# Two expert layers of a one-core kernel: up products per batch as rows are turned, routing placed among them, a bias taken into the shared expert's down product, and later folds

## The reference, cut to what matters

```python
# second layer (E=8 routed experts, I=256, top 2) and one shared expert
s = softmax(z @ gate_w.T); idx = top2(s + gate_b); comb = s where chosen, else 0
up_e = z @ w1[e] + b1[e];  c_e = z @ w3[e] + b3[e];  q = up_e * c_e
g, l = q[..., ::2], q[..., 1::2]
g = min(g, 7); l = clip(l, -7, 7); h_e = g * sigmoid(1.702 * g) * (l + 1)
y = sum_e comb_e * (h_e @ w2[e] + b2[e]) + (shared: h_s @ sw2 + sb2)
x = x + layernorm(y)

# third layer (E=8, F=512, top 2, weights of the two chosen normalised)
y = sum_e comb_e * (silu(z @ W1[e].T) @ W2[e].T);  x = x + layernorm(y)
```

## Time and profile before

| what | value |
|---|---|
| median of three runs | 2537.59 us (2532.54 to 2545.24) |
| profiled execution, its own time | 2533.08 us |
| its span | 2531.3 us, 46421 instructions |
| PE busy | 1916.8 us (76%) |
| PEld busy | 1318.0 us (52%) |
| DVE busy | 1696.1 us (67%) |
| ACT busy | 1089.0 us (43%) |
| POOL busy | 851.6 us (34%) |
| mean granted TensorE clock | 0.859 |

### The profile page before, as it was taken

One profiled execution on the slowest core, in us unless ns is written; L12 is line 12 of the kernel. 1 busy time (PEld: TensorE's weight loads), 2 busy tenths in 40 slices (PEclk: granted clock), 3 DMA queues, 4 the chain that ended last, 5 costly groups with the idle time before them and its releaser, 6 DMA issues. The chain is left out here.

```text
span 2531.3 us, 46421 instructions
## 1 busy us (share of the span) xinstructions
PE 1916.8 (76%) x16420; PEld 1318.0 (52%) x16420; DVE 1696.1 (67%) x4018; ACT 1089.0 (43%) x2022; POOL 851.6 (34%) x630
## 2 busy tenths in 40 slices
PE   5888886587778876449999846878878747999666
PEld 2555554255555553337777614444444336888444
DVE  4777777676555564668999951788887857223574
ACT  2666664354445542204444421555555412333442
POOL 3000000774455430113344333445454319900211
PEclk8999999799999898659999965698888757999678
DMA  3011110200000000010000046566665432000000
GB/s 104 30 39 40 40 38 2 80 16 16 16 16 16 16 16 1 5 22 11 21 21 16 5 133 172 145 175 174 169 178 166 119 122 89 26 8 1 6 1 19
DMA packets 126969, 144.92 MB, mean 57 GB/s; under 512 B 73222, under 2 KB 100673, under 8 KB 123992
## 3 DMA queue, kind: packets, MB, share of 16 engines
q1 hardware_dynamic: 123542, 132.82, 18.9%
q10 hardware_dynamic: 3266, 9.96, 1.0%
HBM read 94.46 MB, written 40.81 MB: 53 GB/s over the span
## 5 line engine op out<-in xcount | busy, mean ns | idle before, releaser
L454 ACT ACTIVATE l0a_pr<-l0a_sm,l0a_nm 128x512 f32<-128x512 f32 x256 | 185.1, 724 | 142.6 <-DVE l0a_nm L367 142.1
L367 DVE CUSTOM_DVE_ANT_0 l0a_sm<-l0a_ps_s,l0a_tb 128x512 f32<-128x512 f32 x256 | 170.8, 685 | 87.6 <-PE l0a_ps_s L522 84.7
L2609 ACT ACTIVATE l2a_pr<-l2a_ps_s,l2a_nm 128x512 f32<-128x512 f32 x256 | 173.8, 685 | 116.6 <-DVE l2a_nm L2528 115.6
L530 PE MATMUL l0a_ps_p<-top_c_ident,l0a_pr 128*128 128x128 f32 x1024 | 168.9, 288 | 54.4 <-ACT l0a_pT L462 54.2
L530 PEld LDWEIGHTS l0a_ps_p<-top_c_ident,l0a_pr 128*128 128x128 f32 x1024 | 109.3, 142 | 116.5 <-ACT l0a_pr L454 65.1
L2528 DVE TENSOR_REDUCE l2a_nm<-l2a_ps_s 128x2 f32<-128x1024 f32 x128 | 156.7, 1224 | 4.4
L2535 DVE STREAM_TRANSPOSE l2a_tt<-l2a_pr 128x1024 f32<-128x1024 f32 x128 | 158.0, 1234 | 0.1
L1557 POOL TENSOR_TENSOR l1f_h<-l1f_lm,l1f_sg 128x512 f32<-128x512 f32 x72 | 92.5, 1285 | 184.9 <-DVE l1f_lm L1626 184.9
L807 POOL TENSOR_TENSOR l0f_ct<-l0f_raw,l0f_cos_scaled 128x1024 f32<-128x1024 f32 x32 | 76.7, 2397 | 174.0 <-issue 94.2
L1929 ACT ACTIVATE l2f_h<-l2f_ps_h 128x512 f32<-128x512 f32 x128 | 76.5, 598 | 135.8 <-PE l2f_ps_h L1474 129.8
L1684 ACT ACTIVATE l1f_csb<-l1f_ps_c,l1f_b3e 128x512 f32<-128x512 f32 x128 | 88.1, 688 | 106.0 <-PE l1f_ps_c L1474 105.7
(11 more groups left out here) (522 smaller groups left out, 5190.5 us busy)
## 6 DMA issues: line engine op xcount, KB each, us to landing
l2a_rawk<-l_k SPq DMA_DIRECT2D x16, 1024.0 KB, 13.3
l2a_qb<-l_qband SPq DMA_DIRECT2D x16, 768.0 KB
l2a_sb<-l_pband SPq DMA_DIRECT2D x32, 384.0 KB
l_qband<-l2a_staged SPq DMA_DIRECT2D x14, 768.0 KB, 15.1
l0a_tb<-l_bias SPq DMA_DIRECT2D x16, 448.0 KB
l2a_ks<-l_k SPq DMA_DIRECT2D x16, 384.0 KB
l_pband<-l2a_pr SPq DMA_DIRECT2D x32, 192.0 KB, 8.7
l_pband<-l2a_pr SPq DMA_DIRECT2D x32, 144.0 KB, 2.2
```

What stands on the lines that cost most here:

```text
L367: v.tensor_tensor_reduce(sm[j % 4][:, :], ps_s[j % 2][:, :], tb[slot][:, off:off + N][:, ::-1], -1.0, 3e38, ALU.add, ALU.min, nm[:, j % 4: ...
L454: a.activation(pr[j % 4][:, :], sm[j % 4][:, :], ACT.Exp, bias=nm[:, j % 4:j % 4 + 1], scale=-1.0).then_inc(m["p_ready"], 1)
L530: last = pe.transpose(ps_p[j % 2][:, tile(k)], pr[j % 4][:, tile(k)], ident[:, :])
L2609: a.activation(pr[slot][:, 2 * (g % 2) + u, :], ps_s[g % 2][:, u, :], ACT.Exp, bias=nm[:, g % 2, u:u + 1], accum_out=rs[:, n % 2, 2 * (g % ...
```

## The change

In both layers the splitting of turned tokens moves between the normalisations of later batches (`Router.tokens`, `Router.split`), weights are masked or stored before the routing, the logits stand after the last turned batch, and the up products wait only for the split of their own batch. In `l1_ffn` the routing weights are turned after the first batch's up products, four products of 36 columns instead of sixteen of 9; ACT copies them. `b2` is a block tile of 36 rows (zeroed on GpSimd, eight loads), one 36-row product per batch opens the shared expert's down product, which then accumulates; `acc` is begun by a copy of this sum instead of by a start value and an add. TensorE's first pair of experts is written out, the others stay in a loop. In `l2_ffn` the fold loads move from ACT's queue to SP's, behind the first two experts' weights; `wcon` is turned after the third batch's up product; GpSimd waits for the first accumulation before the butterflies.

```diff
 class Router:
+    def split(self, v, ch, b):
+        cols = slice(b * N, (b + 1) * N)
+        v.wait_ge(self.zT_ready, b + 1)
+        ch.link(high_part(v, self.zT_masked[:, cols], self.zT[:, cols]))
+        v.tensor_copy(self.zT_high[:, cols], self.zT_masked[:, cols])
+        v.tensor_tensor(self.zT_low[:, cols], ..., ALU.subtract).then_inc(self.parts_ready, 1)
+
+    def tokens(self, v, ch, xs, weights):
+        for b in range(B + 1):
+            if b < B:
+                self.norm.statistics(v, ch, b, lambda t: xs[:, b * NT + t, :])
+            if b:
...
+                self.norm.normalize(v, ch, b - 1, ...)
+                ch.wait()
+                v.sem_inc(self.zb_ready, 1)
+            if b >= 2:
+                self.split(v, ch, b - 2)
+            if b == B:
+                weights()
+        self.split(v, ch, B - 1)
+
+    def route(self, v, ch, ps_gate, ...):
...
 l1_ffn, sync
-                sp.dma_start(b2[0:E, :], w["b2"]).then_inc(biases, 16)
-                sp.dma_start(b2[E:E + 1, :], w["sb2"]...).then_inc(biases, 16)
+                sp.wait_ge(b2_zero, 1)
+                for t in range(NT):
+                    first = t * (E + 1)
+                    sp.dma_start(b2[first:first + E, t, :], w["b2"]).then_inc(b2_loaded, 16)
+                    sp.dma_start(b2[first + E:first + E + 1, t, :], w["sb2"]...).then_inc(b2_loaded, 16)
...
 l1_ffn, vector
-                r.vector(v, ch, xs, ps_gate, gate_b, gate_b_loaded)
-                v.wait_ge(biases, 16 * (2 * (E + 1) + 2))
+                r.tokens(v, ch, xs, lambda: mask_weights(0, 0))
+                r.route(v, ch, ps_gate, gate_b, gate_b_loaded)
                 v.sem_inc(comb_ready, 1)
-                mask_weights(0, 0)
-                for b in range(B):
-                    v.wait_ge(ct_ready, b + 1)
-                    v.tensor_copy(combT[:, b * N:(b + 1) * N], ps_t[0:E + 1, :]).then_inc(combT_ready, 1)
-                for b in range(B):
-                    v.wait_ge(init_ready, b + 1)
-                    v.tensor_copy(acc[:, b * NT:(b + 1) * NT, :], ps_y[b % 2][:, :, :]).then_inc(acc_done, 1)
+                v.wait_ge(biases, 16 * 2 * (E + 1))
...
+                    if shared:
+                        v.tensor_copy(acc[:, b * NT:(b + 1) * NT, :], ps_y[b % 2][:, :, :]).then_inc(acc_done, 1)
+                        return
...
 l1_ffn, scalar
                 for b in range(B):
                     step(0, b, b3[:, 0, :, :])
+                    if b == 0:
+                        a.wait_ge(ct_ready, 1)
+                        a.copy(combT[:, :], ps_t[0:R, :]).then_inc(combT_ready, 1)
...
 l1_ffn, tensor
-                r.tensor(pe, ps_t, ps_gate)
-                pe.wait_ge(comb_ready, 1)
...
+                r.turn(pe, ps_t)
+                r.logits(pe, ps_gate)
...
                 def down(e, b, slot):
+                    if shared:
+                        pe.wait_ge(combT_ready, 1)
+                        pe.wait_ge(b2_loaded, 16 * 2 * NT)
+                        pe.matmul(ps_y[b % 2]..., combT[:, b * P:(b + 1) * P], b2..., start=True, stop=False)
...
                 for b in range(B):
                     up(0, b, 0)
-                    if b:
+                    if b == 0:
+                        pe.wait_ge(comb_ready, 1)
+                        for k in range(B):
+                            last = pe.transpose(ps_t[0:R, k * P:(k + 1) * P], r.comb[:, k * NT:(k + 1) * NT, :]..., ident)
+                        last.then_inc(ct_ready, 1)
+                    else:
                         down(0, b - 1, 0)
...
 l2_ffn, sync: behind load(0), load(1)
+                sp.dma_start(wcon...); sp.dma_start(fold.up[0]...); sp.dma_start(fold.bu[0]...)
+                for i in range(fold.stages):
+                    sp.dma_start(upw[:, i, :], ...); sp.dma_start(dnw[:, j, :], ...)
 l2_ffn, gpsimd
+                g.wait_ge(acc_done, 1)
                 g.wait_ge(first_loaded, 32)
                 g.wait_ge(dn0_ready, 1)
 l2_ffn, vector
-                store_weights(0, 0)
-                r.vector(v, ch, xs, ps_gate, None, normalize=True)
+                r.tokens(v, ch, xs, lambda: store_weights(0, 0))
+                r.route(v, ch, ps_gate, None, normalize=True)
 l2_ffn, scalar
...
-                r.scalar(a, ps_t)
+                r.turned(a, ps_t)
+                r.exponential(a)
                 for b in range(B):
                     step(0, b)
+                    if b == 2:
+                        a.wait_ge(wcon_ps, 1)
+                        a.copy(fold.dn[0][:, :], ps_t[:, :]).then_inc(dn0_ready, 1)
 l2_ffn, tensor
+                r.turn(pe, ps_t)
                 turn_weights(0, 0, 0)
...
-                r.tensor(pe, ps_t, ps_gate)
-                pe.wait_ge(r.parts_ready, B)
+                r.logits(pe, ps_gate)
                 for b in range(B):
+                    pe.wait_ge(r.parts_ready, b + 1)
                     up(0, b, 0)
                     if b:
                         down(0, b - 1, 0)
+                    if b == 2:
...
```

More of the change, by code:

```diff
@@ L1446, in tensor, with logits @@
             last.then_inc(self.t_ready, 1)
+    def logits(self, pe, ps_gate):
         pe.wait_ge(self.zT_ready, B)
@@ L1735, in down @@
                     n = e * B + b
+                    shared = isinstance(e, int) and e == 0
+                    if not (shared and b < 2):
+                        pe.wait_ge(acc_done, n - 1)
+                    if shared:
+                        pe.wait_ge(combT_ready, 1)
+                        pe.wait_ge(b2_loaded, 16 * 2 * NT)
+                        pe.matmul(ps_y[b % 2][:, :, :].rearrange("p t d -> p (t d)"), combT[:, b * P:(b + 1) * P],
+                                  b2[:, :, :].rearrange("p t d -> p (t d)"), start=True, stop=False)
                     pe.wait_ge(h_ready, n * 2 + 2)
-                    pe.wait_ge(acc_done, n + 3)
                     for t in range(NT):
@@ L1740, in down, with expert @@
                             last = pe.matmul(ps_y[b % 2][:, t, :], h[b % 2][:, k, t * P:(t + 1) * P], w2[slot][:, k, :],
[L1741 removed]
+                                             start=(k == 0 and not shared), stop=(k == 1 and (t == NT - 1 or not shared)))
                     last.then_inc(y_ready, 1)
[L1744 removed]
                 for b in range(B):
                     up(0, b, 0)
[L1747 to L1756 removed]
+                    if b == 0:
+                        pe.wait_ge(comb_ready, 1)
+                        for k in range(B):
+                            last = pe.transpose(ps_t[0:R, k * P:(k + 1) * P], r.comb[:, k * NT:(k + 1) * NT, :].rearrange("p t e -> p (t e)"),
+                                                c["ident"][:, :])
+                        last.then_inc(ct_ready, 1)
+                    else:
+                        down(0, b - 1, 0)
+                def expert(e, slot):
+                    for b in range(B):
+                        up(e, b, slot)
+                        if b == 0:
+                            down(e - 1, B - 1, 1 - slot)
+                        else:
+                            down(e, b - 1, slot)
+                expert(1, 1)
+                expert(2, 0)
+                with pe.Fori(1, E // 2) as i:
+                    expert(i * 2 + 1, 1)
+                    expert(i * 2 + 2, 0)
                 down(E, B - 1, 0)
@@ L1982, in _ @@
                         down(0, b - 1, 0)
+                    if b == 2:
+                        pe.wait_ge(wcon_loaded, 16)
+                        for k in range(fold.chunks):
+                            last = pe.transpose(ps_t[:, k * P:(k + 1) * P], wcon[:, k, :], c["ident"][:, :])
+                        last.then_inc(wcon_ps, 1)
                     if b == 1:
```

98 lines of the change are left out of this document (33 added, 65 removed).

## The result

| | before | changed kernel |
|---|---|---|
| median of four runs | 2535.07 us (2532.51 to 2545.24) | 2492.41 us (2491.69 to 2496.87) |
| profiled execution, its own time (span) | 2533.08 (2531.3) us | 2491.87 (2489.7) us |
| PE busy | 1916.8 us (76%) | 1895.2 us (76%) |
| DVE busy | 1696.1 us (67%) | 1665.9 us (67%) |
| ACT busy | 1089.0 us (43%) | 1090.1 us (44%) |

The time ratio is 0.9834, with an interval of 0.9814 to 0.9854: 42 us faster, give or take 5. The forecast was 2500.2 us within 2491 to 2512, 37.4 us faster. A second set of runs of the same changed kernel gave 2493.97 us, ratio 0.9836 (0.9815 to 0.9856). One execution of the kernel before, in the runs beside e9 to e12, took 4245 us and is left out of their ratios.

A forecast was written before the change was run, and what follows sets the result against it. The order of work in the two expert layers' heads was taken as the bound, not engine busy time. Savings of 15.0 (first layer) and 22.4 (second) make 37.4, taken from the 2537.6 median: 2500.2 us, range 2491 to 2512.

The forecast's parts named there:

- The heads are on the path, the loops keep their length: Both expert layers: time saved ahead of the steady loop moves all that follows, and the steady loops keep their length.
- Layer 1, first up product 19.2 earlier: First expert layer's head: first up product starts at 1123.0 instead of 1142.22, with 3 us of slack for the weights.
- First product 15.6 earlier, routing is what comes next: First expert layer: VectorE must finish routing first, so it takes the first product at 1130.4, 15.6 us earlier.
- From the first to the second batch 8.3, bounds 7.0 and 10.5: First expert layer: first to second batch's first product takes 8.3 us, was 8.26; 7.0 at best, 10.5 at low clock.
- Rival (a): First layer: TensorE's 3 us gap drops the clock, shared expert runs half slow, bias products cost 3.4; 2506.5; chance 0.10.
- Bias products 0.5 in all: First layer's shared expert: four products of 0.86 us each, three hidden where VectorE is behind, the fourth mostly paid: 0.5.
- Layer 2, 22.4: Second expert layer: 22.4 us saved (19.5 to 23.5), first up product 23.0 earlier, logits lasting 7.0, `wcon` transposes costing 0.6.
- The three parts of its first up product: Second layer's head, 23.0 earlier: 12.5 waiting for weights, some 12 of GpSimd slowing VectorE, less the logits' new order.
- The fold loads' place on ScalarE, "the layer's gain would be nearer 15": Second layer's head: with the fold loads left on ScalarE, its copy holds the tokens until 2087; gain nearer 15.
- Butterflies from 44 us on, 67 us of cover: Second layer: butterflies start about 44 us after the layer's start and end 67 us before GpSimd is next wanted.
- (b): Second layer starts less early: single-queue loads late or VectorE slowed before the butterflies; 8 to 15 lost, say 2511; chance 0.09.
- (c): Second layer: third expert's weights arrive late behind 10 MB of fold loads on SP; slower than before, about 2545; chance 0.02.

The follow-up runs named there:

- e9: Kernel before, with one wait added: GpSimd starts the second expert layer's butterflies only after the first accumulation; 2521.31 us, ratio 0.9949.
- e12: The changed kernel run again without an edit; 2493.97 us, ratio 0.9836 against the kernel before.
- e1: Changed kernel with only the first expert layer changed, the second layer as before with the old router; 2522.71 us, ratio 0.9959.
- e2: Changed kernel with only the second expert layer changed, the first layer as before with the old router; 2509.39 us, ratio 0.9896.
- e3: Changed kernel with the 21 fold loads back at the head of ScalarE's queue; 2506.14 us, ratio 0.9881 against the kernel before.
- e6: Changed kernel with each bias product moved ahead of the third half of the next up product; 2493.76 us, ratio 0.9820 against the kernel before.
- e7: Changed kernel with twelve unused products filling TensorE's 3.34 us gap in the first layer; 2493.44 us, ratio 0.9831 against the kernel before.
- e5: Changed kernel without the down biases and their four products; 2494.97 us, ratio 0.9827 against the kernel before.
- e10: Changed kernel with seven unused wide products between the token turnings in each layer's head; 2496.24 us, ratio 0.9838 against the kernel before.
- e4: Changed kernel with `wcon` turned ahead of the logits and butterflies not waiting for the first accumulation; 2497.10 us, ratio 0.9851 against the kernel before.
- e8: Changed kernel with each batch's logits made right after the next batch is turned, in both layers; 2493.08 us, ratio 0.9819 against the kernel before.

## Why the prediction was right, point by point

- **The heads are on the path, the loops keep their length.** Right. Both layers' steady parts are within 0.4 us of before, and layer gains pass through to the kernel (e1, e2).
- **Layer 1, first up product 19.2 earlier.** 19.6, with the weights' slack of 3 us at 2.1.
- **First product 15.6 earlier, routing is what comes next.** 15.7. Right, and the timeline shows it: `comb`, then the product. VectorE's count of steps (13.5 for four statistics, four normalisations and two splits) placed the last turning 13.45 us into layer 2.
- **From the first to the second batch 8.3, bounds 7.0 and 10.5.** 7.8 in five of eight profiles with the gap and 9.2 in three (e1, e3, e6); 6.55 without the gap (e7). The bounds held both. Rival (a) had the mechanism right, a gap drops the clock, and had its extent wrong: the clock is back 2.9 us behind the gap in the changed kernel, 5.9 behind it in e1. The Trainium skill (TensorE: Matmul & The Clock Gate, HAM oscillation), on which that rival leant, tells of waits for DMAs that put the array back to the lower clock for the work behind them. The granted clock of 0.50 from 1130 agrees, here behind a wait of 3.34 us for VectorE, and e7 prices it at 1.0 to 2.2 of the layer.
- **Bias products 0.5 in all.** Wrong: 3.4. This is the mis-sized term, and both factors failed. One product costs TensorE 1.25 (1.06 until the down product starts) rather than 0.86. And the cover was read off one place, the fourth batch of the earlier trace rows, and given to three of the four products, but only two lie ahead of it; these cost 0.3 and 0.5. The other two lie where VectorE already waited for operands in the kernel before, and cost 1.3 each. Rival (a) had the same sum, "paid in full (3.4)", by luck: four in full would be 5.0, and it is two in full and a third of the others. Without the products layer 1 would have gained 16.7, against a forecast of 15.5 ahead of this term.
- **Layer 2, 22.4.** 22.9 to 23.9 when the logits last about 7 us (e2, e5, e6, e10, e12), as the sum had it; 26.5 when they last 4.05. All of these are counted from the 276.05 of one profile; against the 279.42 of the same old code in e1 they would be 3.4 more. The logits' duration was taken as fixed from a row at half clock. That TensorE's clock might rise within them was not in the sum nor among the rivals, and it brings 2.6 of the 4.1 us by which the layer beat the forecast in that execution.
- **The three parts of its first up product.** The prediction put 12.5 on the wait for weights and 12 on GpSimd's interference. Holding the butterflies alone brings 13.4 (e9); the rest of the change brings the remaining 10.7 (33.41 to 22.74). But the wait for weights is not what that was: e3 has the tokens ahead of the weights and the butterflies held, and its first up product stands at 34.23, no earlier than e9's. All of the 10.7 needs the fold loads off ScalarE; statistics that start 12.5 earlier bring nothing while the copy behind them is held. The Trainium skill (SBUF — State Buffer, SBUF: two separate sides) calls the port pair that VectorE and GpSimd share an exclusive lock for the length of an instruction; the trace agrees: a split takes 0.68 alone, a butterfly instruction 1.28, and the four splits beside them took 1.74 to 2.01 in the kernel before, 1.76 in e4.
- **The fold loads' place on ScalarE, "the layer's gain would be nearer 15".** 12.5. Right in kind. The rule that issuing elsewhere saves only the usually small time to start a transfer (the Trainium skill, DMA: Bandwidth & Descriptors, Issuing engines are not separate DMA queues) fits the transfers; what it says nothing of is the work queued behind the issues, which the move brought forward by 11.5 us here.
- **Butterflies from 44 us on, 67 us of cover.** 40.9 and 68.1. The wait for the first accumulation was not the last to end: ScalarE's copy of `wcon` (2095.08 + 0.59) was.
- **Rivals (b) and (c).** Neither came: from 2075 to 2305 no row of the changed kernel's timeline shows a wait of any engine that a DMA ended, though SP issues 21 fold loads ahead of the third expert's weights. **Not in the sum:** 1.9 us outside the layers, 0.6 of it ahead of layer 1, within what the unchanged stretches vary by.
- **Against which time.** The sum came to 2495.7 against the profiled execution, 3.8 above that of the changed kernel. The 2500.2 is higher since it was stated against a median of three, 2537.6; the median of four is 2535.07.

The errors partly offset each other, which is luck: -2.9 (bias products), +0.7 (up to the second batch), +0.4 (rest of layer 1), +1.5 (layer 2 with the slower logits), +2.6 (logits' clock), +1.9 (outside) make the +4.2 between 37.4 and 41.6.

## What to carry to other kernels

Slack has to be read in the very interval where the added work will fall: VectorE was 1.0 us behind in one batch and waited for its operand in the next, and of four equal products two were mostly hidden and two paid whole. An engine that issues DMAs is held up for all that stands behind them in its program, so put them on an engine with nothing to do next. Before an order is redone, try the single wait that takes a disturbing engine away: here it alone gave over a third of the whole gain, and, once the order was changed, nearly nothing.

## What the runs showed of the hardware

- The same program, with the same start of its logits, got TensorE's higher clock in one execution 1 us into them and in another not until after them (2072 to 2074: 1.00 against 0.50), though TensorE had done the same work before them in both. In the first it fell again to 0.50 behind the logits, with TensorE busy for all of the 2 us from 2074. A duration read at half clock in a head has two values, 6.84 and 4.05 here, and a single profile shows one.
- A gap of 3.3 us or more lost the clock in all eight profiles of the changed kernel's head that had it, and so did e8's of 2.70 (0.50 from 1128 to 1134), while those of 2.54 of the earlier trace rows went either way. The clock was back 2.9 us behind the gap where this was 3.34, and 5.9 behind it where it was 3.50.
- A product of 36 rows by 512 columns in float32 takes 1.06 us of TensorE at the full clock until the next product starts, no less than the 0.86 of a 128-row one; fewer rows brought nothing here.
- ScalarE loads a table (1.28 us, at 1127.84) ahead of its sigmoid, while it waits for VectorE's first product, so the load is off the path here.
